# Streaming the feed-forward weights with a casting DMA for every tile, in place of a bf16 copy in DRAM made at the start

## What is computed

```python
# attention: every token alone, over its 32 channels of 64
qkv = einsum('nlck,cki->nlci', x.reshape(N, Ls, 32, 64), Wqkv) + bqkv
scores = einsum('nlcd,nled->nldce', q, k) / 8
ctx = einsum('nldcm,nlcd->nldm', softmax(scores), v)
out = einsum('nlck,ko->nlco', ctx.transpose(0, 1, 3, 2), Wout) + bout
# feed-forward: 2048 -> 8192 -> 2048
ffn = (silu(x @ w_gate.T) * (x @ w_up.T)) @ w_down.T
# both between layer norms and with a residual
x = x + layernorm(attn(layernorm(x)))
x = x + layernorm(ffn(layernorm(x)))
```

## Time and profile before

| What | us |
|---|---|
| Median of the runs (2: 5943.98 and 5945.29) | 5944.63 |
| The profiled execution's own time | 5943.41 |
| Its span on the slowest core (core 1) | 5941.9 |
| Spans of all cores | 5921.7 to 5941.9 |
| Matmuls busy (PE), of the span | 3159.3 |
| VectorE busy (DVE) | 3220.4 |
| ScalarE busy (ACT) | 2043.2 |
| GpSimd busy (POOL) | 16.4 |

### The profile page before, as it was taken

The page is one execution under the profiler, slowest core; times in us unless marked ns, Lnnn a source line. Parts: engine busy times, 40 slices in busy tenths (PEclk is TensorE's granted clock), DMA queues, the critical chain, the costliest instruction groups (busy, mean ns, idle before and its releaser), DMA issues.

```text
span 5941.9 us, 47520 instructions; the slowest of 8 cores (5921.7 to 5941.9 us)
## 1 busy us (share of the span) xinstructions
PE 3159.3 (53%) x15536; PEld 1474.1 (25%) x15536; DVE 3220.4 (54%) x3680; ACT 2043.2 (34%) x2953; POOL 16.4 (0%) x34
## 2 busy tenths in 40 slices
PE   1101000103959696318686866068696960499993
PEld 0100000002424333103333432033343320244441
DVE  5682004785856585667666664758565756510112
ACT  3432002434543443234534442244444432221210
POOL 0000000000000000000000000000000000000000
PEclk9955555556979797659898987579797975699996
DMA  9999994002424242114232422133242321244442
GB/s 116 110 108 110 109 108 56 0 7 64 141 59 151 75 128 75 52 32 144 75 128 85 138 75 75 39 103 124 75 138 82 128 69 32 87 153 142 153 138 78
DMA packets 177940, 558.92 MB, mean 94 GB/s; under 512 B 49568, under 2 KB 65952, under 8 KB 174496
## 3 DMA queue, kind: packets, MB, share of 16 engines
q1 hardware_dynamic: 171840, 444.69, 23.2%
q0 software_dynamic: 5856, 111.18, 16.8%
HBM read 641.83 MB, written 125.83 MB: 129 GB/s over the span
## 4 chain that ended last, share of the span: by engine, by line
PE 32%; DVE 29%; issue 12%; ACT 11%; another core or an unknown queue 8%; DMA 7%; DVEq 1%; SPq 0%; ACTq 0%; POOL 0%; POOLq 0%
PE dps L408 12%; PE gps L346 10%; PE ups L356 7%; DVE es_sb L314 6%; DVE zs_sb L744 4%; DMA wd_sb<-wdc 4%; DVE es_sb L729 4%; DVE zs_sb L738 3%; DVE ctx_sb L323 3%; ACT kd_sb L255 2%; DMA x2s_sb<-x2h 2%; PE mps L182 1%; ACT v_sb L292 1%; ACT q_sb L292 1%
## 5 line engine op out<-in xcount | busy, mean ns | idle before, releaser
L346 PE MATMUL gps<-xn_sb,wg_sb 128*128 128x512 bf16 x4096 | 948.0, 385 | 102.9 <-DVE gated_sb L381 87.5
L408 PE MATMUL dps<-gated_sb,wd_sb 128*128 128x512 bf16 x4096 | 930.4, 385 | 85.6 <-DMA wd_sb<-wdc 51.3
L766 ACT ACTIVATE es_sb<-es_sb 128x4096 bf16<-128x4096 bf16 x256 | 922.1, 3602 | 11.5 <-DVE es_sb L729 11.5
L356 PE MATMUL ups<-xn_sb,wu_sb 128*128 128x512 bf16 x4096 | 925.8, 379 | 0.0
L242 PE MATMUL mps<-xn_sb,wqkv_sb 128*128 128x128 bf16 x512 | 72.4, 302 | 1437.4 <-DVE xn_sb L797 1385.9
L755 ACT ACTIVATE rz_sb<-zf_sb 128x128 bf16<-128x128 bf16 x256 | 79.0, 309 | 1858.7 <-DVE zf_sb L748 1858.5
L314 DVE TENSOR_TENSOR es_sb<-es_sb,u_sb 128x4096 bf16<-128x4096 bf16 x256 | 586.8, 2292 | 27.7 <-DVE u_sb L305 1.4
L729 DVE TENSOR_TENSOR es_sb<-q_sb,kd_sb 128x4096 bf16<-128x4096 bf16 x256 | 584.8, 2286 | 8.7 <-DVE ctx_sb L319 0.5
L323 DVE TENSOR_TENSOR ctx_sb<-ctx_sb,es_sb 128x4096 bf16<-128x4096 bf16 x240 | 550.1, 2292 | 26.0 <-DVE es_sb L314 1.4
L346 PEld LDWEIGHTS gps<-xn_sb,wg_sb 128*128 128x128 bf16 x4096 | 400.5, 99 | 620.0 <-issue 168.5
L408 PEld LDWEIGHTS dps<-gated_sb,wd_sb 128*128 128x128 bf16 x4096 | 393.0, 99 | 622.2 <-issue 199.6
(11 more groups left out here) (84 smaller groups left out, 1970.3 us busy)
## 6 DMA issues: line engine op xcount, KB each, us to landing
wg_sb<-wgc SPq DMA_DIRECT2D x256, 512.0 KB, 3.6
wu_sb<-wuc SPq DMA_DIRECT2D x256, 512.0 KB, 3.4
wd_sb<-wdc SPq DMA_DIRECT2D x256, 512.0 KB, 3.3
wgc<-wgH POOLq DMA_DIRECT2D x4, 8192.0 KB, 450.4
wuc<-wuH POOLq DMA_DIRECT2D x4, 8192.0 KB, 527.4
wdc<-wdH POOLq DMA_DIRECT2D x4, 8192.0 KB, 603.8
yT<-outs_sb SPq DMA_DIRECT2D x64, 256.0 KB, 2.7
xb_sb<-xH POOLq DMA_DIRECT2D x16, 512.0 KB, 10.3
```

The costliest lines, as they stand in the source:

```text
L346: return tn.matmul(out=gps[pb].ap(), lhsT=wg_sb[pb].ap()[:, ft * 128:(ft + 1) * 128], rhs=xn2_sb.ap()[:, ft * W:(ft + 1) * W], start=(ft = ...
L356: return tn.matmul(out=ups[pb].ap(), lhsT=wu_sb[pb].ap()[:, ft * 128:(ft + 1) * 128], rhs=xn2_sb.ap()[:, ft * W:(ft + 1) * W], start=(ft = ...
L408: return tn.matmul(out=dps[pb].ap(), lhsT=wd_sb[wb].ap()[:, sh * 128:(sh + 1) * 128], rhs=gated_sb.ap()[:, ht * W:(ht + 1) * W], start=(ht ...
L766: ta = plan.op("A", lambda a, buf=buf: a.activation(out=buf.ap(), in_=buf.ap(), func=AF.Exp, scale=0.125), deps=[last[f"s_{c}_{j}"]], inc="A")
```

## The change

The copies wgc, wuc and wdc and the twelve DMAs that fill them are gone. Every weight tile is instead read from the float32 input and cast to bf16 on its way into SBUF. All 768 of these loads move from SP's queue to POOL's. Buffers, matmuls and the order in which the plan is written stay.

```diff
-    wgc = nc.dram_tensor("wgc", [HID, D], BF16, kind="Internal").ap()
-    wuc = nc.dram_tensor("wuc", [HID, D], BF16, kind="Internal").ap()
-    wdc = nc.dram_tensor("wdc", [HID, D], BF16, kind="Internal").ap()
...
         def d_g(g, h=h, pb=pb):
             return g.dma_start(out=wg_sb[pb].ap(),
-                               in_=wgc[h * 128:(h + 1) * 128, :])
-        tg = plan.op("S", d_g, deps=dep(f"wgfree{pb}", f"wcg{h // 16}"),
-                     inc=f"Dwg{pb}")
+                               in_=wgT[h * 128:(h + 1) * 128, :])
+        tg = plan.op("G", d_g, deps=dep(f"wgfree{pb}"), inc=f"Dwg{pb}")
         def d_u(g, h=h, pb=pb):
             return g.dma_start(out=wu_sb[pb].ap(),
-                               in_=wuc[h * 128:(h + 1) * 128, :])
-        tu_d = plan.op("S", d_u, deps=dep(f"wufree{pb}", f"wcu{h // 16}"),
-                       inc=f"Dwu{pb}")
+                               in_=wuT[h * 128:(h + 1) * 128, :])
+        tu_d = plan.op("G", d_u, deps=dep(f"wufree{pb}"), inc=f"Dwu{pb}")
...
-                                   in_=wdc[r0:r0 + 128, :])
-            td = plan.op("S", d_w,
-                         deps=dep(f"wdfree{wb}", f"wcd{2 * hh + half}"),
+                                   in_=wdT[r0:r0 + 128, :])
+            td = plan.op("G", d_w, deps=dep(f"wdfree{wb}"),
                          inc=f"Dwd{wb}")
...
-    for s in range(4):
-        for name_, dst_, src_ in (("g", wgc, wgT), ("u", wuc, wuT),
-                                  ("d", wdc, wdT)):
-            def fcache(g, dst_=dst_, src_=src_, s=s):
-                return g.dma_start(out=dst_[s * 2048:(s + 1) * 2048, :],
-                                   in_=src_[s * 2048:(s + 1) * 2048, :])
-            last[f"wc{name_}{s}"] = plan.op("G", fcache, inc=f"Dwc{name_}{s}")
```

More of the change, by code:

```diff
@@ L810, in build_program @@
     sems = {name: nc.alloc_semaphore(f"s{name}") for name in plan.counts}
-    qsems = {"G": tuple(["Dcq", "Dco", "Dxb0", "Dxb1", "Dxb2"]
-                        + [f"Dwc{n}{s}" for n in "gud" for s in range(4)]),
+    qsems = {"G": ("Dcq", "Dco", "Dxb0", "Dxb1", "Dxb2",
+                   "Dwg0", "Dwg1", "Dwu0", "Dwu1", "Dwd0", "Dwd1"),
              "S": ("Db", "Dxw", "Dr0", "Dr1", "Do",
-                   "Dxr0", "Dxr1", "Dxr2", "Dxr3",
-                   "Dwg0", "Dwg1", "Dwu0", "Dwu1", "Dwd0", "Dwd1")}
+                   "Dxr0", "Dxr1", "Dxr2", "Dxr3")}
     def run_stream(eng_handle, name):
```

## The result

| What | before | after |
|---|---|---|
| Median of the runs, us (10 and 11, on one chip) | 5954.1 | 5897.7 |
| Ratio after / before, 95% interval | | 0.9905 [0.9885, 0.9925] |
| The profiled execution, us | 5943.4 | 5873.8 |
| Span of core 1, us | 5941.9 | 5834.9 |
| Mean granted clock, all cores | 0.770 to 0.773 | 0.790 to 0.795 |

The gain is real and smaller than 2%. The forecast of 6083 us missed by 3%, and the sign with it; the time lies in the lower part of the stated range of 5790 to 6400 us. A page is that of the slowest core, here core 2.

What follows compares the result with a forecast made beforehand. Bound by start waits behind the copies and by w_down reloads in the down atoms, the kernel was forecast at 5943.4 - 447 + 550 + 9 + 28 = 6083 us, slower by 2.3%, range 5790 to 6400 us.

Steps and rivals of the forecast that it cites:

- The start stage: Start, first quarter: without the copies, the long waits for a spill and a load of x go, -447 us.
- The cycle of the down atoms: Down atoms, two buffers: a pair of tiles takes one matmul group plus one whole reload, 10.8 us with the new load.
- The gate and up tiles: Gate and up atoms: loads fit into 10.35 us but the rate is tight in the tail, +9 us, at most +18.
- The window starts: Four window starts: load of x and first four tiles share DMA engines with sixteen reads, 7 us each, +28 us.
- A tile's load on POOL: Down atoms: a w_down cast load lands in 6.5 us, between 5.6 and 7.3, giving 5.4 us for a tile.
- The clock: Down atoms: PE's 3.7 us gaps may lower its clock; halfway taken, 6.1 us for a tile, +550 us over 234 tiles.
- A: Rival, down atoms: load starts at once, 5.6 us, clock stays up, 4.95 us a tile, 5786 us in all; chance 0.18.
- B: Rival, down atoms: load keeps 7.3 us, clock falls in every gap, 7.2 us a tile, 6340 us in all; chance 0.24.
- C: Rival, every phase: float32 reads lower the rate to 108 GB/s, 4.85 us a tile, about 6640 us; chance 0.06.
- D: Rival, start: the 447 us gain does not come because spills meet other traffic, 6530 us; chance 0.04.

Runs made afterwards that it cites:

- the spread copies: The kernel before, with its twelve copies issued three per slot in slots 0 to 3, behind the load of x: ratio 0.9281, 5509.4 us.

## Why the prediction was wrong

**What held.** The start stage: -447 forecast, -445 measured, and the spread copies confirm the cause. The cycle of the down atoms: group, 0.5 us to POOL's issue, load, 0.14 us. The gate and up tiles: no loss, in the changed kernel and in the one that copies only w_down. The window starts that an attention follows cost 10.8 us each for the 7 taken, inside the bounds, and the cause is the one named, tiles beside the reads. The fourth cost nothing, so that 28 us forecast lie so near the 32 measured is luck: too small a price, times one start too many.

**The step that failed first: "A tile's load on POOL", 6.5 us taken.** The load measures 5.3 us (median, core 1) to 5.7 us (core 2), and 5.6 us in the chain. The step took the middle between the fast load of x, 7.3 us, and the first cast load with idle engines, 5.6 us. It had itself noted that each load of x runs beside a spill of 2048 packets. It should have gone by that: a w_down tile runs beside no spill. The run with x after the spill shows that this alone makes 7.2 into 5.2 us at best. Of queues that share an engine the Trainium skill (DMA: Bandwidth & Descriptors, "Queues, rings and completion order") says that an engine alternates between them packet by packet. The trace agrees, with 2064 small packets beside 2089 large ones in the earlier trace rows. The fit of the same page of the Trainium skill ("Anatomy of one DMA"), which the prediction set aside because no load came near it, gave an estimate of 4.4 us: on core 1 the best load took 5.0 us and the median 5.3, so it was 0.9 us short of the median, and my value 1.2 us over it. In the sum: a pair with 5.6 us in place of 6.5 is 0.9 us shorter, 0.45 us for a tile, times 234 tiles is 105 us.

**The other step that failed, by as much: "The clock", 5.4 raised to 6.1 us for a tile.** Halfway between "holds" and "falls in every gap" added 0.7 us for a tile, 164 us. Measured are 5.1 us for a tile where the chain at full clock gives 4.95, so some 0.2 us; PE's busy time says the same, 7 to 10 us more in a phase of 32 tiles. Three things made it small. With the quicker load most of PE's gaps are 2.0 to 3.2 us, not 3.7. In the down phases of all cores I counted the gaps that follow 16 matmuls at full clock: of 518 gaps of 2.0 to 3.2 us, 200 had 16 matmuls of more than 4.0 us behind them, of 137 longer ones (up to 4.5 us) 111. And a fall costs about 2.0 us even after a gap of 5.9 us, not 2.8, as the kernel with one buffer shows. The two terms together, 105 us and (0.7 - 0.2) x 234 = 117 us, are 222 of the 228 us between +550 and +322. (How they part depends on the load: with the median's 5.3 us in place of the chain's 5.6 it is 140 us for the load and some 90 for the clock.) With both at their measured size the forecast's own sum would have been 5943 - 447 + 328 + 9 + 28 = 5861 us, 0.2% from the profiled 5873.8.

**The rivals.** A, the load that starts at once, was the right one: 5.6 us for the load, 4.95 us for a tile and 158 us for a phase, against 5.1 us and 158 to 172 us measured in undivided phases of cores 1 and 2, save one of 179; its 5786 us missed by 1.5%, as it held the clock at full speed and the window starts at nothing. That its phase comes so near is in part luck: its load was 0.3 us too long for the median, and the clock, which it held, did fall behind some of the gaps. B, C and D are out: the median load took 5.3 us and not 7.3, the rate held at 153 GB/s in the tail, and the start's gain came. (The price of C was also added up wrongly: 6083 + 179 + 403 is 6665 us, not about 6640. Nothing hangs on it.) A had 0.18 and deserved more: it was the only case whose row had nothing else in the DMA queues, as the down phases have not.

## What to carry to other kernels

A load's time is read from a row with the same neighbours in the DMA queues, not only with the same bytes and queue. With two buffers the pace is half of (group + release to landing), so each us of load latency costs half a us per tile as soon as the engine's own pace is passed, and releasing a buffer in halves buys most of that back (here 232 of 322 us in the down phases of core 1). And before a costly staging copy is taken out, ask whether it costs bytes or only stands in front of small transfers that the path waits for: here moving it was worth 7%, removing it 1%, since the cast load that took its place came onto the path.

## What was unexpected

- A half tile of float32 landed no sooner than a whole one (5.6 against 5.3 us in the median), probably since two or more were in flight and the DMA engines 0.88 busy; a half tile of bf16 from SP did (2.6 against 3.3 us).
- Four more cast loads beside sixteen small reads doubled the time of those reads' issues on SP, 25.6 against 12.5 us. The plan itself does this: each read waits for the landing of the read four before it (`d.append(trs[k - 4])`), and SP waited 18.1 us for such landings. So a collision in the DMA engines can show as a long row of issues, and not only as a longer landing.
- With one buffer and gaps of 5.9 us TensorE's clock fell in every gap on core 1, but in more than half of the cases it came back well within the next group of 16 matmuls: of 248 such groups, 133 took under 5.5 us and 83 over 6.3.
- The small packets lost far more than their share: in the stage of the copies a spill of 0.52 MB took 597 us, while the quickest one of before landed in 4.0 us.
